# K, Q and the experts' rows turned by block-permuted transfers and VectorE instead of by identity products

## What is computed

```python
# attention, x: [4, 512, 512], 16 heads of 128
q = rmsnorm((x @ Wq).reshape(B, T, H, D), q_rms_w)
k = rmsnorm((x @ Wk).reshape(B, T, H, D), k_rms_w)
v = (x @ Wv).reshape(B, T, H, D)
scores = einsum('bthd,bshd->bhts', q, k) / sqrt(D) + alibi_bias      # causal
y = rmsnorm(einsum('bhts,bshd->bhtd', softmax(scores), v), subln_w)
x = layernorm(x + y.reshape(B, T, H * D) @ Wproj)
# mixture of 8 experts, the best 2 of each row
top_vals, top_idx = top_k(x @ w_router, 2); probs = softmax(top_vals)
out = sum over the two of  probs * (square(relu(x @ w_fc[e])) @ w_proj[e])
x = layernorm(x + out)
```

## Time and profile before

| | |
|---|---|
| median of 3 runs | 1438.51 us (1438.0 to 1438.63) |
| the profiled execution | 1442.51 us, of which span 1440.7 us |
| TensorE busy | 1400.9 us, 97% of the span |
| VectorE, ScalarE, GpSimd busy | 813.3, 730.3, 424.2 us |
| transfers | 200.45 MB, mean 139 GB/s |
| mean granted TensorE clock | 0.992 |

### The profile page before, as it was taken

The page is one execution under the profiler, slowest core; times in us unless marked ns, Lnnn a source line. Parts: engine busy times, 40 slices in busy tenths (PEclk is TensorE's granted clock), DMA queues, the critical chain, the costliest instruction groups (busy, mean ns, idle before and its releaser), DMA issues. The chain is left out here.

```text
span 1440.7 us, 26432 instructions
## 1 busy us (share of the span) xinstructions
PE 1400.9 (97%) x7744; PEld 1184.6 (82%) x7745; DVE 813.3 (56%) x1877; ACT 730.3 (51%) x1633; POOL 424.2 (29%) x410
## 2 busy tenths in 40 slices
PE   8999999999999999999999999999999989999994
PEld 6888888888888888888888888878887868888783
DVE  6555655656556555555565555567777763333334
ACT  5565656656556566566565565543333223333334
POOL 1212221212112122222121212103445553353565
PEclk9999999999999999999999999999999999999997
DMA  5243333232433333333334245557659546756699
GB/s 185 75 130 95 109 95 115 88 113 91 131 95 109 95 96 108 96 107 109 117 89 115 76 128 157 143 136 171 148 137 233 176 139 247 265 201 230 187 192 237
DMA packets 136851, 200.45 MB, mean 139 GB/s; under 512 B 16624, under 2 KB 83312, under 8 KB 133488
## 3 DMA queue, kind: packets, MB, share of 16 engines
q1 hardware_dynamic: 126032, 149.67, 36.0%
q0 software_dynamic: 10784, 50.36, 11.9%
HBM read 160.05 MB, written 92.62 MB: 175 GB/s over the span
## 5 line engine op out<-in xcount | busy, mean ns | idle before, releaser
L413 POOL TENSOR_TENSOR small<-small,half 128x4 f32<-128x4 f32 x193 | 195.0, 1010 | 764.2 <-DVE small L443 764.2
L557 DVE CUSTOM_DVE_ANT_0 logit<-score_ps,bias 128x128 f32<-128x128 f32 (+3 forms) x256 | 124.8, 487 | 157.1 <-PE score_ps L699 117.6
L347 ACT ACTIVATE prob<-logit,small 128x128 f32<-128x128 f32 (+3 forms) x256 | 144.2, 563 | 120.1 <-DVE small L557 116.5
L712 PEld LDWEIGHTS y_ps<-vs,prob_t 128*128 128x128 f32 x1280 | 175.1, 191 | 21.5 <-ACT prob_t L354 4.5
L712 PE MATMUL y_ps<-vs,prob_t 128*128 (+1 forms) x1280 | 185.6, 276 | 0.7 <-ACT prob_t L354 0.7
L354 ACT ACTIVATE prob_t<-prob_ps 128x128 f32<-128x128 f32 (+3 forms) x256 | 111.5, 436 | 54.9 <-PE prob_ps L705 53.9
L705 PE MATMUL prob_ps<-ident,prob 128*128 128x128 f32 x640 | 112.8, 274 | 3.2 <-ACT prob L347 2.8
L443 DVE TENSOR_REDUCE small<-squares 128x4 f32<-128x516 f32 x128 | 88.4, 691 | 45.7 <-ACT squares L269 43.8
L631 PE MATMUL v_ps<-w_hi,x_hi 128*128 (+1 forms) x256 | 106.7, 417 | 1.4 <-DVE w_lo L488 1.4
L929 ACT ACTIVATE yt_hi<-x_raw,subln 128x512 fp32r<-128x512 f32 x60 | 43.2, 723 | 126.2 <-DVE x_raw L1025 51.2
L631 PE MATMUL v_ps<-w_hi,x_lo 128*128 (+1 forms) x256 | 106.6, 416 | 0.0
(11 more groups left out here) (233 smaller groups left out, 3370.0 us busy)
## 6 DMA issues: line engine op xcount, KB each, us to landing
slots_x<-in_zeros SPq DMA_DIRECT2D x64, 512.0 KB, 4.4
y_scratch<-x_now SPq DMA_DIRECT2D x65, 256.0 KB, 2.8
x_raw<-in_x_t SPq DMA_DIRECT2D x64, 256.0 KB, 2.6
slots_y<-in_zeros SPq DMA_DIRECT2D x64, 256.0 KB, 4.4
y_raw<-y_scratch SPq DMA_DIRECT2D x56, 256.0 KB
w_raw<-in_w_experts POOLq DMA_DIRECT2D x7, 2048.0 KB
w_hi<-in_w_experts POOLq DMA_DIRECT2D x7, 2048.0 KB
w_raw<-in_w_all SPq DMA_DIRECT2D x16, 768.0 KB, 6.1
```

Of the source, the lines that this page charges most:

```text
L347: nc.scalar.activation(prob[:, 0:width], logit[:, 0:width], ACT.Exp, scale=-1.0, bias=least[:, h:h + 1], accum_out=row_sum[:, (i % 2) * HG ...
L413: nc.gpsimd.tensor_tensor(r, ms, half[:, :], ALU.pow).then_inc(ready, 1)
L557: nc.vector.tensor_tensor_reduce(out=logit[:, 0:width], in0=score_ps[:, 0:width], in1=bias[:, h, T - width:T], scale=1.0, scalar=3e38, op0 ...
L712: mm = nc.tensor.matmul(y_ps[:, :].rearrange("p (b h i) -> p h b i", b=QB, h=HG)[:, h, :, :], prob_t[:, j * P:(j + 1) * P], one(vs[:, bass ...
```

## The change

**Attention.** K and Q are no longer turned on TensorE. VectorE writes the normalised K and Q into one buffer `kq` (128x1024) in 32-column blocks; SP stores it to DRAM (`store_kq`, 512 KB); SP then waits for that store to land and loads it back in four transfers of 128 KB with the row and column blocks exchanged (`load_kq`, runs of 1 KB); VectorE transposes inside 32x32 blocks (`turn_part`, one instruction each for K and Q) and so completes the turn, in SBUF. The projections run one tile further ahead: in step n they make tile n+2, and the turns in step n are those of tile n+1, made in step n-1. The projections of tile 1 (36 matmuls) go ahead of step 0, and the last two steps have none. The output projections `project_y` that stood in the last step are spread over the last two. K's, Q's and y's squares share one buffer `sq`, with waits between them. The splits of the next round's weights move between steps: ScalarE rounds block 0 in step i = 0 and blocks 1 and 2 in step i = 1.

**Experts.** SP loads the rows of a slot in four transfers, again with the blocks exchanged (runs of 512 B), into four buffers instead of two, six slots ahead; VectorE's block transpose (`turn_x`) takes the place of TensorE's four identity products. The rows of the up weights are permuted to match on the host. `turn_hid` stays on TensorE. Ahead of the third slot TensorE runs 46 filler products (`keep_busy`) instead of 10.

The core of the diff:

```diff
+            def store_kq(t):
+                sp.wait_ge(k_normed, t + 1)
+                sp.wait_ge(q_normed, t + 1)
+                if not (isinstance(t, int) and t == 1):
+                    sp.nop(nofuse=True)
+                    sp.wait_ge(kq_loaded, (t - 1) * (16 * QB))
+                sp.dma_start(kq_scratch, kq[:, :]).then_inc(kq_stored, 16)
+
+            def load_kq(t):
+                sp.wait_ge(kq_stored, t * 16)
+                sp.nop(nofuse=True)
+                sp.wait_ge(k_turned, t)
+                sp.wait_ge(q_turned, t)
+                rows = kq_scratch.rearrange("(a j) (b c) -> b j a c", a=QB, b=QB)
+                for b in range(QB):
+                    sp.dma_start(kq_in[b * QP:(b + 1) * QP, :].rearrange("p (a c) -> p a c", a=QB), rows[b])\
+                        .then_inc(kq_loaded, 16)
...
+            def normalise_part(m, src, r, ready, count, done):
+                dve.wait_ge(ready, count)
+                if not (isinstance(count, int) and count == 2):
+                    dve.wait_ge(kq_stored, (count - 2) * 16)
+                nc.vector.tensor_tensor(kq_parts[:, m], src[:, :].rearrange("p (h b i) -> p h b i", h=HG, b=QB),
+                                        r.unsqueeze(2).unsqueeze(3).to_broadcast([P, HG, QB, QP]), ALU.mult)\
+                    .then_inc(done, 1)
+
+            def turn_part(m, out, t, ready, done):
+                dve.wait_ge(kq_loaded, t * (16 * QB))
+                dve.wait_ge(ready, t)
+                nc.vector.transpose(turned_columns(out), in_parts[:, m]).then_inc(done, 1)
 
...
                     logits(2)
                     if ahead:
-                        normalise(qn[:, :], q_ps, q_r, q_rstd, n + 2, q_normed)
-                    else:
-                        split_y(2)
+                        turn_part(1, kt, n + 1, k_ready, k_turned)
+                    if i > 0 and ahead:
+                        turn_part(0, qt, n + 1, q_ready, q_turned)
+                    if projects:
+                        normalise_part(0, q_ps, q_r, q_rstd, n + 3, q_normed)
+                    if not ahead:
                         split_y(3)
-                    if last and i == TB - 2:
+                    if last and i == TB - 3:
                         turn_y(1)
                     logits(3)
-                    if last and i == TB - 2:
+                    if i == 0:
+                        turn_part(0, qt, n + 1, q_ready, q_turned)
+                    if last and i == TB - 3:
                         split_y(0)
                         split_y(1)
...
+                        pe.wait_ge(x_ready, n + 3)
+                        pe.wait_ge(k_normed, n + 2)
+                        if i == TB - 2:
...
-                    if ahead:
-                        pe.wait_ge(k_normed, n + 2)
-                        if i == 0:
-                            pe.wait_ge(k_ready, n + 1)
-                        turn(kt_ps, kn, k_turned)
+                    if projects:
+                        if i == TB - 2:
+                            pe.wait_ge(w_ready, it * 3 + CT * 3 + 3)
                         project(v_ps, 2, xb, wp, 0, 4)
...
                         project(v_ps, 2, xb, wp, 4, 8)
-                        pe.wait_ge(q_normed, n + 2)
-                        turn(qt_ps, qn[:, :], q_turned)
-                    else:
...
+        def load_row_blocks(engine, at, y, blocks):
+            for u in blocks:
+                engine.dma_start(xs[y][u * QP:(u + 1) * QP, :].rearrange("p (a c) -> p a c", a=QB),
+                                 x_slots[bass.ds(at, 1), u, :, :, :].rearrange("o j a c -> (o j) a c"))\
+                    .then_inc(xs_loaded[y], 16)
...
+            def turn_x(b, y, loaded, split=None):
+                dve.wait_ge(xs_loaded[y], loaded)
+                if split is not None:
+                    dve.wait_ge(xt_ready, split)
+                nc.vector.transpose(turned_columns(xt[b]), xs[y]).then_inc(xs_turned, 1)
...
             row_shifts()
+            row_places()
+            turn_x(0, 2, 16 * QB, 1)
             split_x(0, 3)
-            row_places()
+            turn_x(1, 3, 16 * QB, 2)
             square(0, 3)
             split_x(1, 4)
+            turn_x(0, 0, 32 * QB, 3)
 
             def slot_step(k, b, h, y, q):
                 split_hid(b, k)
+                if more(k, 2):
...
-            keep_busy(h_ps[1], 10)
+            keep_busy(h_ps[1], 46)
             up(0, second, 3)
-            turn_x(1, 32)
...
             def slot_step(k, b, h, y, q):
                 turn_hid(b, k)
...
-                if more(k, 2):
-                    turn_x(b, h * 16 + 32)
                 down(b, load_owner(k), k)
```

356 lines of the change are left out of this document (206 added, 150 removed).

## The result

The change made the kernel slower: 1447.06 us in the median of 7 runs (1443.99 to 1451.49) against 1438.63 (7 runs, 1437.61 to 1442.05), a ratio of 1.005 with a 95% interval of 1.0033 to 1.0066. I had forecast 1408 and gave a slowdown 7 in 100, for another reason than the one that came. The profiled execution took 1447.06 us, its span 1445.4.

What follows compares the result with a forecast made beforehand. TensorE, busy 97%, was taken as the bound. Steps 25.8, last round 2.9, set-up −8.3, first load −1.5, routing 0.8, experts 11: 30.7 us off 1442.5 gives 1411.8, adjusted by 4.0 to 1408; range 1395 to 1425 (8 in 10).

Steps and rivals of the forecast that it cites:

- a slowdown 7 in 100: Rival, attention steps: the K and Q trip through DRAM lands late and stalls VectorE's turns; 1470 us at T = 13; chance 0.07.
- tiles 2 and 3: Attention steps of these tiles: VectorE's idle time covers the new turns, gaining 0.75 and 0.87 us per step.
- tile 0: Attention steps of tile 0: Q's turn lengthens VectorE's chain, a loss of 0.2 us; TensorE's wait becomes 1.3 us.
- the experts: Expert stage: TensorE's last slot 12 us earlier, of which 11 arrive because the end hangs on GpSimd; bounds 7 and 14.
- the last round: Last four attention steps: −0.2, −2.2, +1.3 and +3.9, together +2.9 us gained; bounds 0 and 8.3.
- the seam: Stretch between last round and projection: no cost of its own forecast; the account's line with routing has +0.8 us.
- Tile 1: Attention steps of tile 1: the chain to Q's low part lets `score(0)` come at 512.7, a gain of 0.3 us.
- The round trip: K and Q through DRAM in the attention: about 9.3 us, hidden with 2 us spare, costed at nothing.
- the last of them ends as before: Experts, GpSimd: its last weight split still ends at 1353.7 us; then 32 gathers take 59 us, 1413 at the earliest.
- The clock: Rival: TensorE's 1.3 us waits in steps of tile 0 lower its clock, costing 27 us: 1435 us; chance 0.08.
- my four: The rivals: VectorE's chain takes all (0.12), lowered clock (0.08), all 72 us come off (0.04), late round trip (0.07).
- VectorE's chain takes all: Rival, steps of tiles 0 and 1: added ops cost 0.5 us more, 15 us less gain, 1423 us; chance 0.12.

Runs made afterwards that it cites:

- f2_cover_too: Changed kernel with Q's rounding earlier in tile 0, turned expert rows in PSUM, zeroing in the last round's third step, and matmuls cut 12, 9, 5, 5, 5: 1416.12 us.
- filler8: Changed kernel with eight identity products as pure filler put back in each step that has projections, where the turns of K and Q stood: 1471.51 us.
- v552: Changed kernel with the 12 matmuls of V's projection split 5, 5, 2 over the gaps instead of 4, 4, 4: 1458.86 us.
- cover: Changed kernel with projection matmuls cut 12, 9, 5, 5, 5 over a step's gaps, ScalarE and VectorE pieces moved along, Q's rounding earlier in tile 0: 1430.19 us.
- q0_order: Changed kernel with ScalarE's rounding of Q in steps of tile 0 put ahead of the copy of head 3's turned probabilities: 1442.06 us.
- notrip: Changed kernel without the transfers of K and Q through DRAM, semaphores raised at once: step lengths unchanged, run 1452.05 us.
- f2_filler8: f2_cover_too with the eight filler identity products of filler8 put back per step: 1442.67 us.

## Why the prediction was wrong

**The step that failed** is the one on tiles 2 and 3: "At logits(3) VectorE has been idle 1.40 and 2.09 us for TensorE's score, which covers two turns in tile 3 whole and in tile 2 nearly: +0.75 and +0.87." Measured: +0.31 and +0.54. Over 15 rounds that is 11.6 of the 35 us by which the sum was off; tile 0 makes 5.9, the experts 10.1, the last round and the seam 6.4. I asked whether VectorE had time for its new work, and it had. I did not ask what the old work had covered on TensorE. The products of K stood between head 2's score and the turn of its probabilities, those of Q between head 3's, and there the head's own chain (logits on VectorE, softmax on ScalarE) comes back to TensorE. A step of tile 3 before, ScalarE's softmax of head 2 and TensorE's turn of it:

```profile
538.76 0.72 ACT L347 ACTIVATE prob<-logit,small 128x512 f32<-128x512 f32 x1 [0.94 <-DVE small L557]
```

```profile
539.97 0.60 PE L705 MATMUL prob_ps<-ident,prob 128*128 128x128 f32 x4
```

And after:

```profile
602.25 0.72 ACT L390 ACTIVATE prob<-logit,small 128x512 f32<-128x512 f32 x1 [0.94 <-DVE small L629]
```

```profile
603.12 0.66 PE L790 MATMUL prob_ps<-ident,prob 128*128 128x128 f32 x4
```

Before, the softmax ended 0.49 us ahead of the turn (539.48 to 539.97); after, 0.15 (602.97 to 603.12), which is the hand-over, the time from one engine's end to the start of the other. The list of waits understates it, since TensorE's matmuls still run when it begins: the row shows no idle time, only a later start. It can be seen in the loads of the weights. Before, the load for the turn ran 0.11 us ahead of its matmul:

```profile
539.86 0.47 PEld L705 LDWEIGHTS prob_ps<-ident,prob 128*128 128x128 f32 x4
```

And after, it started with it, 0.15 behind the softmax:

```profile
603.12 0.42 PEld L790 LDWEIGHTS prob_ps<-ident,prob 128*128 128x128 f32 x4
```

In tile 3 this is the whole shortfall. From the start of `attend(1)` to score(3), with the turn of head 2 between them, TensorE takes 1.40 us for 1.24, and at head 3's place the same again (medians of the rounds): 0.32 of the 0.33 us by which tile 3 fell short of the forecast. In tile 2 the two places cost 0.13 and 0.12. Another 0.25 us is lost there at the start of the step, where I had put nothing. With the change K's projection for the next round stands in this step and no longer in the one after it, and it needs a block of weights that VectorE splits at the end of the step before:

```profile
576.38 0.68 DVE L622 TENSOR_TENSOR w_lo<-w_raw,w_hi  x1
```

```profile
577.42 0.49 PE L710 MATMUL k_ps<-w_hi,x_hi 128*128 x1
```

The split ends at 577.06, 0.36 us before K's first matmul, and in f2_cover_too, where that split is later still, the distance is again 0.36. K's first matmul comes 0.73 us after `score(0)` instead of 0.61 and the first turn of probabilities at 3.63 instead of 3.38; in filler8 they stand at 0.61 and 3.42. So of the 0.56 us that tile 2 lies above TensorE's own work, 0.25 are this wait and 0.25 the two places. filler8 shows that the waiting is there (the filler cost 0.59 and 0.40 of 0.87), v552 and cover that it follows the cut of the work and, in tile 3, goes where the gaps are evened out.

**Tile 1** was right in number (13.09 for 13.01) and in the chain that I named: the low part of Q ends 0.23 us before the next `score(0)`. But it was luck as well. TensorE lost 0.51 us at head 2's place and 0.11 at head 3's, of which the forecast knew nothing, and its own path ends just when that chain does. **Tile 0** was wrong by 0.39, and q0_order shows by what: ScalarE's rounding of Q stands behind keep_prob_t(3). I had written the chain as if it started when Q was turned. With the order put right the step took 12.27; I had said 12.33. Of TensorE's waits there only 0.78 us stand at `score(0)`, where I had put 1.3; 0.47 and 0.09 stand at the turns of heads 2 and 3.

**The round trip** was right in what matters, with notrip as proof, and too long: 2.7 for the store, about 1.3 for the first three issues and 3.0 for the last landing make 7 us, not 9.3. **The last round** missed 3.1 us, 2.6 of them in its first step: I took over its wait for the weight load as it was, and it grew from 1.87 to 4.76. The load is asked for no earlier, it is issued later. Before:

```profile
888.78 1.00 SPq L222 DMA_DIRECT2D w_raw<-in_w_all  x1
```

And after:

```profile
893.10 0.34 SPq L227 DMA_DIRECT2D kq_scratch<-kq  x1
...
894.34 0.73 SPq L249 DMA_DIRECT2D w_raw<-in_w_all  x1
```

The round's first score is at 894.57 before and at 897.50 after, so the issue comes 5.8 us ahead of it before and 3.2 after, since the new store of K and Q stands in front of it on SP and waits for both to be normalised. From the issue to ScalarE's rounding it takes 15.0 and 14.9 us. **The seam** I had at nothing: VectorE's turn of the last early block waits 1.98 us for its load, part of which the change issues in the last step; after it comes a stretch at a lower clock (0.96 from 960 to 1000, 1.00 before). This was read from the trace, not tried, and about 1 us of it is within what two traces differ by.

**The experts.** Slots came 6.06 us apart for 6.04, and GpSimd was the bound, as forecast. The term that was mis-sized is its chain: "the last of them ends as before". The eight splits of an expert took 11.3 to 11.9 us instead of 10.4 to 11.0, 6 us over seven experts, and of the gathers 12 took 1.75 to 1.85 instead of 1.54, together 3. The first gather started 2.2 us after the last split, where I had put nothing. These three make up what was missed. I had this as a bound of 4 us, and put the blame on transposes or small runs. It was the split that came to read both operands from SBUF, an operation that the diff leaves as it is but for the name of its operand. TensorE's last slot was only 6.5 us earlier against the first weight split, not 12. By the fourth slot it had lost 5.0 us where I had put 2.1: it waited 1.8, 2.1 and 1.3 us, and the granted clock was 0.51 from 1195 to 1200 us. That cost nothing, since no gather behind the first had more than 0.3 us ahead of it.

**The rivals.** The clock didn't fall in the steps, and the trip was never late; the slowdown came by none of my four. Nearest was the first, VectorE's chain takes all, at 1423, but its mechanism is right for tile 0 alone, and there the 0.4 us are ScalarE's order.

**Slips in the working.** The four steps of the last round add up to 2.8, not 2.9. In tile 0 the way from 556.0 over 0.69 to 556.95 holds a hand-over of 0.2 that it doesn't name. Neither changes the outcome.

**What stays open:** how the loss between the last round and the first weight split divides, since single traces differ there by more than its parts; what the moved pieces of ScalarE and VectorE do in cover; and why, of the slow gathers, every second one is slow without meeting the split of the rows.

## What to carry to other kernels

Before taking work off a busy engine, ask of each piece what latency it covered: find the next instruction on that engine that needs another engine's answer, and look how long before it that answer was ready. Here the answer came 0.49 us early, of which 0.15 are the hand-over, so 0.34 could be taken and 0.44 were. The work off the path pays only once what remains is cut anew over the gaps, and until then filler of known cost tells whether the engine waits (filler8 and f2_filler8 tell the two states apart at the price of one run each). And when an operand moves from PSUM to SBUF, count its readers: the one that now has two SBUF operands slows its neighbour. Last, a new transfer delays what stands behind it in the same queue, and work that now starts a step earlier needs its inputs a step earlier.

## What the hardware showed that I had not expected

VectorE's block transpose writes to PSUM at 718 ns for 128x512, hardly slower than to SBUF (703). A store of 512 KB from SBUF in rows of 4 KB landed in 2.7 us, while the zeroing transfers of the same size took 4.3 in the same kernel. And indirect gathers on GpSimd slow down too: 12 of 32 took 1.75 to 1.85 us instead of 1.54 while VectorE's split read two SBUF operands, and 2 when it read one from PSUM. The slow ones come in pairs; the first of each (1.83 to 1.85) overlaps the split, the second does not.
